# Attention weighing split into two column halves per key tile, with two score pieces and two first-pass pieces behind each half

## The reference, cut to what matters

```python
xn = layernorm(x)
q, k, v = (xn @ W.T + b).reshape(4, 2048, 16 heads, 16)       # q * 16**-0.5
probs = softmax(einsum('bqhd,bkhd->bhqk', q, k))              # 64 heads (4 x 16), 2048 x 2048 each
attention = einsum('bhqk,bkhd->bqhd', probs, v) @ Wo.T + bo
out = x + attention + mixture_of_experts(xn)                  # 16 experts, top 2, own top-k over tokens
```

## Time and profile before

| | |
|---|---|
| median of 3 runs | 3329.87 us (3329.33 to 3333.35) |
| profiled execution, span | 3325.6 us; the launch's 4.3 us around it are the median less this span |
| PE, PEld, DVE, ACT, POOL busy | 98%, 51%, 86%, 76%, 28% |
| granted PE clock | 1.0 of full speed nearly throughout (mean 0.997) |

### The profile page before, as it was taken

The page is one execution under the profiler, slowest core; times in us unless marked ns, Lnnn a source line. Parts: engine busy times, 40 slices in busy tenths (PEclk is TensorE's granted clock), DMA queues, the critical chain, the costliest instruction groups (busy, mean ns, idle before and its releaser), DMA issues. The chain is left out here.

```text
span 3325.6 us, 68210 instructions
## 1 busy us (share of the span) xinstructions
PE 3272.2 (98%) x20848; PEld 1696.8 (51%) x20848; DVE 2868.3 (86%) x3022; ACT 2516.8 (76%) x5655; POOL 947.6 (28%) x1403
## 2 busy tenths in 40 slices
PE   7999999999999999999999999999999999899999
PEld 6444444444444444444444444444444444488887
DVE  7758999999999999999999999999999999566666
ACT  3558888888888888888888888888888888644443
POOL 2550222222222222222222222222222222344444
PEclk9999999999999999999999999999999999999999
DMA  6783333333333333333333333333333332355554
GB/s 201 204 237 52 58 57 57 57 56 58 55 55 60 58 57 56 57 57 57 55 55 55 55 55 55 55 55 55 55 55 55 55 55 62 110 161 160 166 160 123
DMA packets 139843, 271.64 MB, mean 82 GB/s; under 512 B 30144, under 2 KB 75264, under 8 KB 127296
## 3 DMA queue, kind: packets, MB, share of 16 engines
q1 hardware_dynamic: 137472, 266.71, 37.7%
q10 hardware_dynamic: 2112, 1.35, 0.1%
HBM read 173.59 MB, written 84.93 MB: 78 GB/s over the span
## 5 line engine op out<-in xcount | busy, mean ns | idle before, releaser
L959 DVE TENSOR_REDUCE half_max<-m_ps 128x1 f32<-128x1024 f32 x2006 | 2366.8, 1220 | 193.4 <-PE m_ps L886 188.8
L853 ACT ACTIVATE prob<-s_ps 128x512 f32<-128x512 f32 (+1 forms) x5120 | 2187.4, 522 | 404.4 <-PE s_ps L896 398.5
L896 PE MATMUL s_ps<-q_feat,k_feat 50*128 50x512 f32 (+1 forms) x5120 | 1535.0, 396 | 4.9 <-ACTq L843 2.1
L886 PE MATMUL m_ps<-k_feat,q_feat 48*128 48x512 f32 x4012 | 1358.3, 443 | 7.4
L896 PEld LDWEIGHTS s_ps<-q_feat,k_feat 50*128 50x128 f32 x5120 | 798.7, 184 | 977.4 <-ACT prob L853 869.1
L905 PE MATMUL a_ps<-prob,v_head 128*32 128x512 f32 x8192 | 1091.5, 605 | 0.0
L886 PEld LDWEIGHTS m_ps<-k_feat,q_feat 48*128 48x128 f32 x4012 | 594.9, 185 | 215.6 <-DVE half_max L959 214.1
L905 PEld LDWEIGHTS a_ps<-prob,v_head 128*32 128x32 f32 x8192 | 161.3, 108 | 249.2 <-issue 230.4
L695 POOL CAST shift<-row_max 128x16 fp32r<-128x16 f32 x63 | 12.3, 195 | 945.0 <-DVE row_max L961 945.0
L688 POOL COPY v_head<-v_all 128x256 f32 (+1 forms) x64 | 25.3, 397 | 826.1 <-PE a_ps L905 826.0
L1233 ACT ACTIVATE g_hi<-g 128x512 fp32r<-128x512 f32 x128 | 81.0, 633 | 212.5 <-DVE g L1266 172.1
(11 more groups left out here) (146 smaller groups left out, 2001.7 us busy)
## 6 DMA issues: line engine op xcount, KB each, us to landing
q_feat<-q_parts SPq DMA_DIRECT2D x384, 128.0 KB, 4.2
k_feat<-k_parts SPq DMA_DIRECT2D x384, 128.0 KB, 5.6
q_parts<-parts SPq DMA_DIRECT2D x32, 512.0 KB, 4.5
k_parts<-parts SPq DMA_DIRECT2D x32, 512.0 KB, 4.6
att_dram<-att SPq DMA_DIRECT2D x64, 256.0 KB, 6.4
mask_bc<-mask_b SPq DMA_DIRECT2D x128, 128.0 KB, 4.4
x_in<-in_x SPq DMA_DIRECT2D x16, 512.0 KB, 4.1
xn_dram<-xn SPq DMA_DIRECT2D x16, 512.0 KB, 4.8
```

The lines of the kernel that those rows point to most:

```text
L853: act.activation(prob[tile(r, kt) % R][:, cols(j)], s_ps[slot(r, kt, j) % R][:, wide(j)], ACT.Exp).then_inc(exped, 1)
L886: ins = pe.matmul(m_ps[p % 2][:, k * BLK:(k + 1) * BLK], q_feat[r % 2][LOW, qt * P:(qt + 1) * P], k_feat[r % 2][LOW, key:key + BLK], start ...
L896: pe.matmul(s_ps[slot(r, kt, j) % R][:, wide(j)], k_feat[r % 2][UP, kt * P:(kt + 1) * P], q_feat[r % 2][UP, cols(j)], start=True, stop=Tru ...
L959: dve.tensor_reduce(half_max[r][:, p // 2, p % 2:p % 2 + 1], m_ps[p % 2][:, :], AX.X, ALU.max).then_inc(maxed, 1)
```

## The change

Each key tile's weighing is cut in two: columns 0 to 255 of each query block, then columns 256 to 511. Behind each half stand two score pieces of 512 columns, each followed by one first-pass piece of 512 columns. So a key tile now has four score pieces in place of five, and its order is: half weighing, score 0, first pass, score 1, first pass, half weighing, score 2, first pass, score 3, first pass. The maxima stay 1024 columns wide, two for each query tile; `piece` is now counted for each 512 columns and no longer for each pair. The lag of two key tiles stays. The first half of the weighing carries the waits. `collect` moves behind the last exponential of key tile 1 (before: the third of its five). The end of the accumulation is unchanged: the last two key tiles of the last head are weighed whole.

The diff, cut to its core (the parts in `project` that do the first heads' first pass early are changed in the same manner and keep their order):

```diff
-PAIRS = ST * 2
-EARLY = 10
+PIECES = ST * 4
+OPS = ST * 2
+EARLY = 5
...
+MAX_BANKS = (2, 2)
+def max_op(qt, j):
+    return qt * 2 + j // 2
...
-    CUTS = (0, BLK, 2 * BLK, 3 * BLK, 3 * BLK + BLK // 2, S)
-    NP = len(CUTS) - 1
+    TURN_AT = 2
+    NP = QB
+    CUT = BLK // 2
...
-                        if not first and (kt, j) == (LAG - 1, 2):
+                        if not first and (kt, j) == (1, NP - 1):
                             collect(g - 1)
...
+            def pass1(n, it, r, i):
+                qt, j = divmod(i, 4)
+                if i == 0:
+                    wait_fed(r, it, fed_low)
+                if j % 2 == 0:
+                    pe.wait_ge(maxed, n * OPS + max_op(qt, j) + 1)
+                pe.matmul(m_ps[j // 2][:, (j % 2) * BLK:(j % 2 + 1) * BLK], q_feat[r % 2][LOW, qt * P:(qt + 1) * P],
+                          k_feat[r % 2][LOW, j * BLK:(j + 1) * BLK], start=True, stop=True).then_inc(piece, 1)
...
-            def weigh(g, r, kt):
+            def weigh(g, r, kt, lo=0, hi=BLK):
+                if lo == 0:
+                    if kt == 0:
+                        pe.wait_ge(v_ready, g + 1)
+                        pe.wait_ge(att_read, g + 1)
+                    pe.wait_ge(exped, slot(g, kt, NP - 1) + 1 + R)
                 for qb in range(QB):
+                    ins = pe.matmul(a_ps[qb * VW:(qb + 1) * VW, lo:hi], v_head[r % R][:, kt, :],
+                                    prob[tile(r, kt) % R][:, qb * BLK + lo:qb * BLK + hi],
+                                    start=(kt == 0 and lo == 0), stop=(kt == ST - 1 and hi == BLK))
+                if hi == BLK:
+                    ins.then_inc(weighed, 1)
...
                 for kt in range(ST):
-                    a, b = half(kt, 0), half(kt, 1)
-                    score(g, it, r, kt, 0)
-                    a(0)
-                    a(1)
-                    score(g, it, r, kt, 1)
-                    score(g, it, r, kt, 2)
-                    if kt >= LAG:
-                        weigh(g, r, kt - LAG)
-                    elif not first:
-                        weigh(g - 1, r - 1, ST + kt - LAG)
-                    score(g, it, r, kt, 3)
-                    b(0)
-                    score(g, it, r, kt, 4)
-                    b(1)
+                    for half in range(2):
+                        weigh_behind(kt - 2, half * CUT, (half + 1) * CUT)
+                        for j in (2 * half, 2 * half + 1):
+                            score(g, it, r, kt, j)
+                            shift_key(4 * kt + j)
...
+                for qt in range(lo, ST):
+                    last_key = 0
+                    for o, banks in enumerate(MAX_BANKS):
+                        if (qt, o) == (turn_at, 1):
+                            turn_shift(n - 1)
+                        last_key += banks
+                        dve.wait_ge(piece, n * PIECES + qt * 4 + last_key)
```

More of the change, by code:

```diff
@@ L442, in first_pass @@
             def first_pass(n, p):
-                if p == 0:
-                    pe.wait_ge(fed_low[n], 16 * LOADS)
-                pe.wait_ge(maxed, n * PAIRS + p + 1)
                 qt, half = divmod(p, 2)
                 for k in range(2):
[L448 to L451, removed]
+                    j = half * 2 + k
+                    if p == 0 and k == 0:
+                        pe.wait_ge(fed_low[n], 16 * LOADS)
+                    if j % 2 == 0:
+                        pe.wait_ge(maxed, n * OPS + max_op(qt, j) + 1)
+                    pe.matmul(m_ps[half][:, k * BLK:(k + 1) * BLK], q_feat[n][low, qt * P:(qt + 1) * P],
+                              k_feat[n][low, j * BLK:(j + 1) * BLK], start=True, stop=True).then_inc(piece, 1)
             with pe.Fori(0, BEFORE) as blk:
@@ new lines, in step, with shift_key, weigh_behind @@
+            def step(g, it, r, first=False, following=True, after=True):
+                def shift_key(i):
+                    i += 4 * EARLY
+                    if i < PIECES and following:
+                        pass1(g + 1, it, r + 1, i)
+                    if i >= PIECES and after:
+                        pass1(g + 2, it, r + 2, i - PIECES)
+                def weigh_behind(kt, lo=0, hi=BLK):
+                    if kt >= 0:
+                        weigh(g, r, kt, lo, hi)
+                    elif not first:
+                        weigh(g - 1, r - 1, ST + kt, lo, hi)
+                for kt in range(ST):
+                    for half in range(2):
[3 more added lines that the diff above has]
+                            shift_key(4 * kt + j)
@@ L940, in _ @@
                 step(g, 0, g, following=g + 1 < HEADS, after=g + 2 < HEADS)
-            for kt in range(ST - LAG, ST):
-                weigh(HEADS - 1, HEADS - 1, kt)
+            weigh(HEADS - 1, HEADS - 1, ST - 2)
+            weigh(HEADS - 1, HEADS - 1, ST - 1)
         @block.vector
```

67 lines of the change are left out of this document (25 added, 42 removed).

## The result

| | before | changed |
|---|---|---|
| median | 3331.26 us (4 runs, 3329.33 to 3333.35) | 3443.34 us |
| all runs | | 3427.58, 3393.69, 3459.09, 3491.38 us |
| mean granted clock of these runs | | 0.962, 0.974, 0.951, 0.943 |
| profiled execution, span | 3325.6 us, clock 0.997 | 3425.8 us (time 3427.58 us), clock 0.962 |

The medians stand at 1.034; the ratio 1.0239 [1.0187, 1.0292] counts only the two lower of the four runs, those of the fast state. All four follow one line. Their mean clocks tell that they spent some 240, 156, 319 and 378 us more at half clock than the kernel before did (an estimate: twice the missing share of the clock, times the span), and their spans are 100, 66, 132 and 164 us longer: 0.41 to 0.43 us for each of those.

The account below looks back on a forecast made before the run. A PE-ACT-PE chain with the whole weighing in it, 2.55 us a tile, bounds the kernel. A head of 16 x 2.46 + 1.49 = 40.85 us against 41.04 gives about 3317, stated as 3318 us; range 3270 to 3365.

Parts of the forecast that it names:

- The half weighing and the stage: PE's key tile: a half weighing takes 0.57 us, the stage between 0.66 us, a tile 2.46 us against 2.55.
- Rival 1: Entry and exit of 2048 half weighings: a half takes 0.60 to 0.62 us, time 3380 to 3420 us; 16%.
- rival 2: Half weighing on PE: it takes only 0.55 us, saving 41 us, time 3277 us; 9%.
- rival 5: DVE keeps the present pattern, idling 0.20 us a tile; period stays 2.55 us, time 3409 us; 4%.
- rival 4: PE's weight loads in the open: 0.08 to 0.11 us per added half, time 3400 to 3431 us; 3%.
- two more increments a tile: Semaphore counts of pieces: by the skill page's 26.3 ns each they would add some 54 us; forecast costs them nothing.
- What would wait: Half tile of 1.23 us: ACT leaves the chain, DVE's maxima fit at 1.14 us, PE alone bounds the tile.
- no load of a score should wait for ACT: Sign in the steady state: score loads on PE don't wait for ACT's exponentials, the release being met by 0.13 us.
- The added wait's length: Each head's first weighing, key tile 2: PE waits 1.49 us for the copy in 63 heads, 94 us.
- Rival 3: Wait for the copy at a head's first weighing costs nothing or little: time 3224 us; 5%.
- no change 0.19: Chance given to the time staying unchanged, with rival 6 and the edges of Rival 1 included.
- Rival 6: Both parts do nothing, weighing and copy both covered: time 3330 us; 4%.

Follow-up runs that it names:

- copy_early: Changed kernel with the accumulator copy (collect) on ACT behind the second exponential of key tile 1, not the fourth: 3262.48 us, 0.9801 of before.
- filler_all: Changed kernel with PE repeating first-pass matmuls while each head's first weighing waits for the copy, the last head included: 3335.97 us, 1.0009 of before.
- before_copy_late: Kernel before, with only the copy moved on ACT from behind the third exponential of key tile 1 to key tile 2's third: 3541.51 us, 1.063.
- copy_mid_again: Same kernel as copy_mid, run once more with a profile to catch its slower level: 3329.61 us.
- copy_mid: Changed kernel with the copy behind the third exponential of key tile 1 in place of the fourth: median 3330.25 us, 0.9985 of before.
- weigh_later: Changed kernel, copy behind key tile 1's third exponential, key tile 2's weighing whole and behind its first two scores: 3348.26 us, 1.0053 of before.

## Why the prediction was wrong

**The half weighing and the stage: right.** 0.57 and 0.66 us, a tile 2.466 us over many, against 2.46. Rival 1 (a dearer half) and rival 2 (a cheaper one) are out, and so is rival 5: DVE left the old pattern. The bounds were 0.55 and 0.78, and the value nearest to the row of the same operation was the right one. Of rival 4 the rows show all eight loads of a half in 0.16 us beside its passes. The Trainium skill, "TensorE: Matmul & The Clock Gate", Part 3, would have open loads in each half; the trace disagrees again. Nor do its increments of 26.3 ns show: four first-pass pieces of a tile are counted where two pairs were, and the half tile is as long as worked out without them. (The prediction's two more increments a tile forget that the fifth score's goes: one more, and by the page's figure 27 us in place of 54, an estimate.)

**What would wait: right in the main.** At full clock no wait of a score for ACT holds PE up. The view of waits seems to say otherwise, for the changed kernel:

```profile
PEld s_ps L909 <- ACT prob L869: 855.7, 1971, 0.8
PEld a_ps L919 <- issue: 543.9, 1143, 1.9
PEld a_ps L919 <- ACT prob L869: 333.5, 903, 1.4
```

The first row reads like the earlier trace rows, but each such load starts 0.57 us after a half weighing, exactly as those put down to "issue" do; the loads' idle time is the weighing, and ACT is only the last event that the profile found. The forecast that "no load of a score should wait for ACT" can't be read from this view; the spacing of the weighings answers it. DVE does not idle 0.1 us ahead of each maximum as I said: its rows are 1.22 us long and one starts every 1.23 us, so that none of the room shows as idle time. The room is there all the same, since two maxima can start 1.14 us apart.

**The added wait's length: right.** 2.77 - 1.23 = 1.54 us from weighing to weighing beyond the usual, against 1.49; 0.05 us over, since the restart lies 0.10 us behind the copy's end and not 0.05. PE's 63 stops are 92.8 us, near the 94 forecast, though they stand under "issue" and not under `att`. So a full-clock head is 41.01 us (median) against 40.85: 0.10 from tiles and 0.05 from the wait. Rival 3 (the wait costs nothing) is out: copy_early shows that its removal gives 1.2 us a head.

**The step that failed is the price of the added wait**, "1.49 us for each of 63 heads, 94 us", with the rows' clock of 1.00 assumed for all the rest of the sum. The wait is the only place, but for the loop's entry, where PE stands for more than 0.4 us among the heads, and I asked what is queued behind it but not what PE's standing still does to PE. It costs its length, 93 us, and the clock besides: 92 us in the profiled executions and 107 in the medians (3443.3 against filler_all's 3336.0). With PE kept busy in the wait, as in filler_all, nothing of the clock's part is left, and the sum is still low: its span is 3334.3 us against 3313, of which (41.05 - 40.85) x 63 = 13 us come from the heads and 8 from a longer start (288.9 against 280.5). The forecast's mechanism, two effects that cancel, then stands, with "same" for its outcome. Two smaller terms: the 4.3 us around the span were 1.7 to 1.8 us in the four runs of the changed kernel, and "no change 0.19" is low by its own terms, which are 0.16 and 0.04 before any edge of rival 1.

The Trainium skill had a warning that I left unused: "TensorE: Matmul & The Clock Gate", on HAM oscillation, tells of a kernel in which waits between bursts of matmuls put the engine to half rate again and again. The trace agrees in kind; its example waits 3 to 5 us for DMAs, here 1.47 us for another engine is enough, so that the page's case would have raised the question and not given the answer.

**Rival 6** (nothing happens) came nearest in its number for the kernel at full clock, from the wrong reason: both parts act, and cancel.

**What stays open.** Why 42 of 63 stops of 1.51 us in before_copy_late are followed by a fall, 11 of 63 stops of 1.47 us in the changed kernel, and in copy_mid_again one of 63 of 0.98 us, and in copy_mid's profile none. The falls are not strewn evenly: in the changed kernel's profile the ten ahead of the last head come in five pairs (at 634 and 689 us, 1317 and 1365, 1618 and 1672, 2126 and 2170, 2624 and 2669), the second always at the next head's stop. Why a stretch lasts 3 us or 65. That the last head stays at half clock to its end goes with its missing first pass, but no run separates the two. And whether the stop at weigh_later's branch is a matter of fetching code; the runs show only that it goes with where the loop's code lies.

## What to carry to other kernels

When an edit moves the producer of a wait, ask first how long the bound engine will stand still in one piece, and count PE's idle stretches beside their sum: here a stop of 1.5 us per 41 us cost its own length and about as much again in clock. Copies that free an accumulator belong as early on their engine as their input allows; moving one by two exponentials was worth 5% of this kernel, more than the restructuring itself. Compare the clock's row and a count of finished tiles before the busy shares, and after any edit to a long hand-written loop look at the branch that closes it.

## What the hardware showed that I had not expected

- Single stops of PE of 1.47 to 1.51 us, once in 41 to 42 us of otherwise dense work, were followed within 3.5 us of their start by a granted clock of 0.50 in 11 of 63 cases and in 42 of 63; stops of 0.98 us in none, but for the last head in one of two profiles.
- In a head without a first pass the clock, once down, stayed down to its end: 64.9 us in the changed kernel, 68.3 us in copy_mid_again, 58.0 us in before_copy_late.
- The same loop-closing branch took 0.36 to 0.37, 0.94 to 1.49, or 5.0 to 5.9 us, by the place of the loop's code alone, and the longest brought a fall of the clock in 9 of 9 cases.
- Eight fp32 matmuls of 256 columns (two passes over four column groups) occupy PE for 0.57 us; of 512 columns 1.00 us.
